# Attention and router kernel on one core: router rows turned on TensorE, a second probabilities' buffer, and norms and tail weighting moved off VectorE

## The chip, the cores and the metric

The kernel runs on one core of a Trainium2 chip. The time is the device time of one execution, in microseconds (us). A core has TensorE (PE in the rows; PEld is its weight load), VectorE (DVE), ScalarE (ACT), GpSimd (POOL) and SyncE (SP), which only issues DMAs. Each engine runs its own list of instructions in order, and the lists are tied together by semaphores that an instruction raises and another engine's instruction waits for.

## What is computed

```python
x = x + xattn(ctx, ctx, layernorm(x))     # 4096 queries of width 512, 3202 keys, one head
x = x + ffn(layernorm(x))                 # 16 experts, the two best of each row, 512 rows an expert at most
# xattn: softmax(q Wq^T (k Wk^T)^T / sqrt(512)) (v Wv^T) Wo^T + biases
# ffn:   gate_probs = softmax(x w_router); each row goes to its two best experts:
#        (silu(x w_gate) * (x w_fc)) w_proj, weighted by the two probabilities
```

## The kernel before

Three blocks run one after the other: `setup` (weights folded into keys `kT` and values `vv`), `attend` (attention and routing, the part that the change touches), and `experts`. `attend` takes the queries in NT = 32 tiles of 128. The 3202 keys are NK = 25 tiles of 128 and a tail of 2. All large products are three passes in f16 of high and low halves (`three_passes`, L45 to L47).

The work is pipelined over steps. In step t:

- TensorE computes the scores of query tile t + 1 (7 chunks of up to 4 key tiles into the banks `sc`), then the tail's scores, then `times_values(t)`: 25 key tiles (k = 0 to 24) of probabilities times values into `acc`. Between these it does small things at fixed places: `row_sum(t)` after k = 0, `greatest(t + 1)` (L1234, the turn of the maxima) after k = 8, `spread(t + 1)` (L1240, the maxima spread to all partitions) after k = 10, `logits(t - 1)` (L1274, L1277, the router's product of tile t - 1) after k = 16. `places(t - 2)` (L1284) stands after the first chunk of scores.
- ScalarE copies the chunks of scores to `s_T` (`copied`, L899), with `rows_high(t - 1)` (L925) after chunk 2 and `query_high(t + 2)` (L936) after chunk 4, then `tail_exp` (L905), the exponentials in three groups of key tiles (L910), and the high halves of the probabilities `pT` (`high`, L919), the last of them after `router_sum(t - 1)` (L929).
- VectorE starts a step with `residual(t - 1)` (L1045 twice, for the two tail keys, and L1048, then the statistics up to L1055). It goes on with the running maximum over the 7 chunks (`maximum`, L999), between which stand `place(t - 2)` (L1104 to L1122, after chunk 1), `normed` and `rows_low(t - 1)` (L1059, L1063, after chunk 2), `row_blocks(t - 1)` (L1067, a transpose in 32 x 32 blocks, after chunk 3) and three parts of `query(t + 2)` (L1128 to L1132, L1135 and L1137, L1140, after chunks 3, 4 and 5). Then come `inverse(t)` (L1029 to L1037), `shift(t + 1)` (the last of the maximum L1004 and L1006, L1008 to L1016, the subtraction L1019 in three groups), `route(t - 1)` (L1086 to L1098) and the low halves of the probabilities (`low`, L1025, three groups).
- GpSimd does `deviation(t - 1)` (L831), `add_bias(t)` (L827: `xb = x_in + bo_row`), `scatter(t - 2)` (L837 to L844, two indirect DMAs), `deviation_q(t + 2)` (L850) and `sums(t + 1)` (L858 six times, L860, L863: the row sums of the exponentials, the first of which waits for the first group of exponentials).
- SyncE loads and stores. The normed rows reach the router transposed through DRAM: `row_blocks` turns 32 x 32 blocks, one DMA stores them to `blocks_r`, and four DMAs load them block by block into `xrT`, which `logits` reads. The queries take the same way through `blocks_q` to `qt`.

So the order on each engine is written out by hand. The places that matter here are these two, `add_bias` before the sums on GpSimd, and the wait at the head of `logits` on TensorE:

```python
if post: deviation(t - 1); add_bias(t)        # GpSimd, step t
if post and placed: scatter(t - 2)
if more_q: deviation_q(t + 2)
if more: sums(t + 1, 1 - h)
...
pe.wait_ge(r_in, 16 * NB * (t + 1))           # TensorE, logits(t)
```

Of the kernel before, what the change touches and what calls it, by code (L numbers as in the profile page):

```python
# [21 lines left out]
ALU = mybir.AluOpType  # L22
# [572 lines left out]
def attend(nc, v):  # L595
# [24 lines left out]
    with ExitStack() as c_:  # L620
# [4 lines left out]
        pT = buf("pT", [P, 2, NK, P], F16)  # L625
# [9 lines left out]
        p_held = buf("p_held", [P, TAIL], F32)  # L635
# [9 lines left out]
        row_bl = buf("row_bl", [P, 2 * D], F16)  # L645
# [40 lines left out]
        ps_y = c_.enter_context(nc.psum_tensor("ps_y", [P, 512], F32))  # L686

# [10 lines left out]
        rb_rdy, rb_out, r_in = sem("rb_rdy"), sem("rb_out"), sem("r_in")  # L698
        qb_rdy, qb_out = sem("qb_rdy"), sem("qb_out")
        rinv_rdy = sem("rinv_rdy")  # L700
# [26 lines left out]
        with nc.Block() as block:  # L727
            @block.sync
            def _(sp):
# [21 lines left out]
                def store_row_blocks(t):  # L751
                    sp.wait_ge(rb_rdy, t + 1)
                    sp.dma_start(blocks_r, row_bl[:]).then_inc(rb_out, 16)

                def load_row_blocks(t):
                    sp.wait_ge(rb_out, 16 * (t + 1))
                    blocks_in(xrT, blocks_r, r_in)

# [13 lines left out]
                def step(t, post, more_x, more_q, turn_q):  # L772
                    if more_x:
                        sp.wait_ge(xb_rdy, t + 1)
                        load_x(t + 1)
                    if post:
                        store_x1(t - 1)
                        store_rows(t - 1)
                        store_row_blocks(t - 1)
                    if more_q:  # L780
                        load_xq(t + 3)
                    if post:
                        load_row_blocks(t - 1)
                    if turn_q:
                        turn_query(t + 2)
# [10 lines left out]
                store_row_blocks(NT - 1)  # L796
                load_row_blocks(NT - 1)
                sp.wait_ge(x1_out, 16 * NT)
                sp.wait_ge(r_out, 16 * NT)
                sp.wait_ge(r_in, 16 * NB * NT)  # L800
# [3 lines left out]
            def _(pool):  # L804
# [71 lines left out]
                add_bias(0)  # L876
# [14 lines left out]
            def _(act):  # L891
# [21 lines left out]
                def high(t, h, g):  # L913

                    a, b = groups[g]
                    act.wait_ge(ex_rdy, NG * t + g + 1)
                    if not isinstance(t, int) or t > 0:
                        act.wait_ge(pv_part, NG * (t - 1) + g + 1)
                    act.activation(pT[:, 0, a:b, :], s_T[h][:, a:b, :], ACT.Copy).then_inc(p_hi, 1)  # L919

                def rows_high(t):
                    act.wait_ge(xs_rdy, t + 1)
                    wait_for(act, r_out, 16 * t)
                    wait_for(act, rb_rdy, t)
                    act.activation(row16[:, 0:D], xs2[:], ACT.Copy, scale=XN_S).then_inc(xs_hi, 1)  # L925
# [7 lines left out]
                def query_high(t):  # L933
                    act.wait_ge(q_xs, t - 1)
                    wait_for(act, qb_rdy, t - 2)
                    act.activation(q16[:, 0:D], xqs[:], ACT.Copy, scale=XN_S).then_inc(q_hi, 1)  # L936

                def step(t, h, post, more, more_q, copies=True):
                    for c in range(NCH if more and copies else 0):
                        copied(t + 1, 1 - h, c)  # L940
                        if c == 2 and post:
                            rows_high(t - 1)
                        if c == 4 and more_q:
                            query_high(t + 2)
                    if post and not more:
                        rows_high(t - 1)
                    if more:
                        tail_exp(t + 1)
                        exponentials(t + 1, 1 - h, 0)
                        exponentials(t + 1, 1 - h, 1)  # L950
                        high(t + 1, 1 - h, 0)
                    if more:
# [33 lines left out]
                rows_high(NT - 1)  # L986
                router_sum(NT - 1)
# [3 lines left out]
            def _(dve):  # L991
# [30 lines left out]
                def low(t, h, g):  # L1022
                    a, b = groups[g]
                    dve.wait_ge(p_hi, NG * t + g + 1)
                    dve.tensor_tensor(pT[:, 1, a:b, :], s_T[h][:, a:b, :], pT[:, 0, a:b, :], ALU.subtract).then_inc(p_lo, 1)  # L1025

                def inverse(t):
                    dve.wait_ge(pt_rdy, t + 1)
                    dve.tensor_tensor(rs_v[:], p_tail[:, 0:1], p_tail[:, 1:2], ALU.add)  # L1029
                    dve.tensor_copy(p_held[:], p_tail[:])  # L1030
# [6 lines left out]
                    dve.reciprocal(rinv[:], rs_v[:]).then_inc(rinv_rdy, 1)  # L1037

                def residual(t):
# [4 lines left out]
                    for i in range(TAIL):  # L1044
                        dve.scalar_tensor_tensor(out=x1[:], in0=v_tail[:, i, :], scalar=p_held[:, i:i + 1],  # L1045
                                                 in1=x1[:] if i else acc[:], op0=ALU.mult, op1=ALU.add)
                        dve.drain()
                    dve.scalar_tensor_tensor(out=x1[:], in0=x1[:], scalar=rinv[:], in1=xb[:],  # L1048
# [6 lines left out]
                    dve.tensor_scalar(var_e[:], mv[:, 1:2], EPS, None, ALU.add).then_inc(mv_rdy, 1)  # L1055

                def normed(t):
                    dve.wait_ge(rs_rdy, t + 1)
                    dve.tensor_scalar(xs2[:], x1[:], mv[:, 0:1], rstd[:], ALU.subtract, ALU.mult).then_inc(xs_rdy, 1)  # L1059

                def rows_low(t):
                    dve.wait_ge(xs_hi, t + 1)
                    dve.scalar_tensor_tensor(out=row16[:, D:2 * D], in0=xs2[:], scalar=XN_S, in1=row16[:, 0:D],  # L1063
                                             op0=ALU.mult, op1=ALU.subtract).then_inc(xs_lo, 1)

                def row_blocks(t):
                    dve.transpose(row_bl[:], row16[:]).then_inc(rb_rdy, 1)  # L1067
# [56 lines left out]
                def query(t, c):  # L1124

                    if c == 3:
                        dve.wait_ge(q_ld, 16 * (t - 1))
# [5 lines left out]
                    if c == 4:  # L1133
                        dve.wait_ge(q_rstd, t - 1)
                        dve.tensor_scalar(shift_q[:], mv_q[:, 0:1], rstd_q[:], 1.0, ALU.mult, ALU.subtract)  # L1135
                        dve.drain()
                        dve.tensor_scalar(xqs[:], xq[:], rstd_q[:], shift_q[:], ALU.mult, ALU.subtract).then_inc(q_xs, 1)  # L1137
# [5 lines left out]
                def step(t, h, post, more, more_q, placed=True):  # L1143
                    if post:
                        residual(t - 1)
                    for c in range(NCH if more else 0):
# [3 lines left out]
                        if c == 2 and post:  # L1150
                            normed(t - 1)
                            rows_low(t - 1)
                        if c == 3 and post:
                            row_blocks(t - 1)
                        if more_q:
                            query(t + 2, c)
                    if not more:
                        place(t - 2)
                        normed(t - 1)
                        rows_low(t - 1)  # L1160
                        dve.drain()
                        row_blocks(t - 1)
# [32 lines left out]
                normed(NT - 1)  # L1195
                rows_low(NT - 1)
                dve.drain()
                row_blocks(NT - 1)
# [7 lines left out]
            def _(pe):  # L1206
# [40 lines left out]
                def times_values(t, post, more):  # L1247
                    wait_for(pe, x1_rdy, t)
                    ends = [b - 1 for a, b in groups]
                    for k in range(NK):  # L1250
# [3 lines left out]
                        last = three_passes(pe, acc[:], (pT[:, 0, k, :], pT[:, 1, k, :]),  # L1254
# [14 lines left out]
                def logits(t):  # L1269

                    pe.wait_ge(r_in, 16 * NB * (t + 1))
# [16 lines left out]
                def step(t, post, more, placed=True):  # L1288
# [8 lines left out]
                    times_values(t, post, more)  # L1297
# [14 lines left out]
                times_values(0, False, True)  # L1312
                step(1, True, True, False)
                with pe.Fori(2, NT - 2) as t:
                    step(t, True, True)
                step(NT - 2, True, True)
                step(NT - 1, True, False)
# [519 lines left out]
```

## Time and profile before

| | us |
|---|---|
| median of three executions | 1792.59 |
| lowest and highest | 1790.32, 1793.38 |
| the profiled execution | 1790.13 |
| its span, first to last instruction | 1788.4 |

| engine | busy, us | share of the span |
|---|---|---|
| TensorE | 1611.5 | 90% |
| VectorE | 1248.5 | 70% |
| ScalarE | 589.9 | 33% |
| GpSimd | 744.9 | 42% |

The span is cut in three: `setup` to about 196 us, `attend` to about 1424 us, `experts` for the rest. A row of a timeline gives the start in us from the span's start, the duration in us, the engine, the line of the kernel, the operation, its output and inputs, how many are merged (x3), and in brackets how long the engine had stood idle before it and whose work ended that wait. A row of a line's instructions gives least, median and greatest duration in ns.

### The profile page before, as it was taken

The page shows a single profiled execution, that of the slowest core. Times are in us where ns is not written, and L with a number is a line of the kernel's source. Part 1 is how long each engine was busy: PE and PEld are TensorE (multiplying, and loading weights), DVE is VectorE, ACT ScalarE, POOL GpSimd, SP SyncE. Part 2 cuts the span into 40 slices and gives each one's busy share as a digit, 9 for nine tenths or more (in the row PEclk, how much of TensorE's full clock was granted, in tenths as well). Part 3 has the DMA queues.
Part 4 walks back from the last instruction along what each step waited for, and adds up shares of the span by engine and source line. Part 5 has one row for each costly group of instructions (what it writes and reads, how often), then busy time and mean ns, then how long its engine had stood idle before and what let it go on. Part 6 is the DMA issues. An engine that isn't in the chain of part 4 may idle for free. (4 is left out here: it accounts for less than half of the span.)

```text
span 1788.4 us, 40760 instructions
## 1 busy us (share of the span) xinstructions
PE 1611.5 (90%) x15565; PEld 1058.9 (59%) x15565; DVE 1248.5 (70%) x2427; ACT 589.9 (33%) x902; POOL 744.9 (42%) x708
## 2 busy tenths in 40 slices
PE   8999989899998999999999899998998369999974
PEld 4444867667766667666776666776665135555430
DVE  4443277888888888888888888888888365555524
ACT  2343233233232332323323233232332025454430
POOL 0100054355443454434544345444455245665540
PEclk9999999999999999999999999999999679999985
DMA  4310112332223322233222322223221268989969
GB/s 153 90 48 7 55 29 66 62 53 47 49 69 59 59 47 47 68 62 59 47 48 70 59 58 47 47 65 64 55 45 37 43 187 186 218 202 217 199 86 375
DMA packets 339922, 155.75 MB, mean 87 GB/s; under 512 B 268642, under 2 KB 285026, under 8 KB 339876
## 3 DMA queue, kind: packets, MB, share of 16 engines
q1 hardware_dynamic: 317424, 111.05, 25.8%
q0 software_dynamic: 16896, 35.42, 10.4%
q10 hardware_dynamic: 5556, 8.66, 1.3%
q8 instruction: 29, 0.48, 0.1%
q14 instruction: 17, 0.14, 0.0%
HBM read 95.04 MB, written 60.06 MB: 87 GB/s over the span
## 5 line engine op out<-in xcount | busy, mean ns | idle before, releaser
L45 PE MATMUL sc<-qt,kT 128*128 128x128 f16 x3100 | 524.5, 219 | 3.8 <-POOL before L821 3.4
L46 PE MATMUL sc<-qt,kT 128*128 128x128 f16 x3100 | 524.4, 219 | 0.0
L47 PE MATMUL sc<-qt,kT 128*128 128x128 f16 x3100 | 524.3, 219 | 0.0
L45 PE MATMUL acc<-vv,pT 128*128 128x512 f16 x800 | 312.7, 391 | 14.3 <-DVE pT L1025 7.8
L46 PE MATMUL acc<-vv,pT 128*128 128x512 f16 x800 | 312.6, 391 | 0.0
L47 PE MATMUL acc<-vv,pT 128*128 128x512 f16 x800 | 312.0, 390 | 0.0
L45 PEld LDWEIGHTS sc<-qt,kT 128*128 128x128 f16 x3100 | 303.6, 98 | 10.4 <-POOL before L821 3.9
L46 PEld LDWEIGHTS sc<-qt,kT 128*128 128x128 f16 x3100 | 303.7, 98 | 3.5
L47 PEld LDWEIGHTS sc<-qt,kT 128*128 128x128 f16 x3100 | 303.7, 98 | 0.0
L858 POOL TENSOR_TENSOR sum<-s_T 128x512 f32<-128x512 f32 x32 | 72.7, 2273 | 378.7 <-ACT s_T L910 378.7
L858 POOL TENSOR_TENSOR sum<-sum,s_T 128x512 f32<-128x512 f32 (+1 forms) x160 | 209.5, 1309 | 31.5 <-issue 16.8
L899 ACT ACTIVATE s_T<-sc 128x512 f32<-128x512 f32 (+1 forms) x224 | 115.3, 541 | 130.4 <-PE sc L47 130.2
L999 DVE TENSOR_TENSOR rm<-rm,s_T 128x512 f32<-128x512 f32 (+1 forms) x160 | 100.5, 628 | 62.5 <-ACT s_T L899 44.7
L1477 POOL DMA_INDIRECT y_dram<-o_sb,sidx x64 | 102.5, 1601 | 99.0 <-ACT o_sb L1520 83.3
L1025 DVE TENSOR_TENSOR pT<-s_T,pT 128x1024 f16<-128x1024 f32 (+1 forms) x96 | 141.0, 1517 | 3.2 <-ACT pT L919 3.2
L910 ACT ACTIVATE s_T<-s_T,e_bias 128x1024 f32<-128x1024 f32 (+1 forms) x96 | 112.8, 1180 | 88.2 <-DVE s_T L1019 88.2
L45 PEld LDWEIGHTS acc<-vv,pT 128*128 128x128 f16 x800 | 84.5, 106 | 94.1 <-issue 14.0
L47 PEld LDWEIGHTS acc<-vv,pT 128*128 128x128 f16 x800 | 80.1, 100 | 100.8 <-issue 11.1
L46 PEld LDWEIGHTS acc<-vv,pT 128*128 128x128 f16 x800 | 79.9, 100 | 80.8 <-issue 5.3
L1019 DVE TENSOR_TENSOR s_T<-s_T,m_b 128x1024 f32<-128x1024 f32 (+1 forms) x96 | 116.1, 1265 | 2.9
L919 ACT ACTIVATE pT<-s_T 128x1024 f16<-128x1024 f32 (+1 forms) x96 | 103.4, 1077 | 1.9 <-PE acc L47 1.9
L844 POOL DMA_INDIRECT tbl_dram<-tok,idx x64 | 73.7, 1151 | 36.7 <-issue 36.7
(292 smaller groups left out, 2849.7 us busy)
## 6 DMA issues: line engine op xcount, KB each, us to landing
xq<-in_x_dram SPq DMA_DIRECT2D x32, 256.0 KB, 2.9
x_in<-in_x_dram SPq DMA_DIRECT2D x32, 256.0 KB, 2.8
raw_g<-in_L_ffn_w_gate_dram SPq DMA_DIRECT2D x16, 512.0 KB
raw_f<-in_L_ffn_w_fc_dram SPq DMA_DIRECT2D x16, 512.0 KB
raw_p<-in_L_ffn_w_proj_dram SPq DMA_DIRECT2D x16, 512.0 KB
y_dram<-x SPq DMA_DIRECT2D x32, 256.0 KB
rows_dram<-row SPq DMA_DIRECT2D x32, 256.0 KB
blocks_r<-row_bl SPq DMA_DIRECT2D x32, 256.0 KB, 2.0
```

Source lines behind the costliest of these rows:

```text
L45: pe.matmul(out, s_hi, m_hi, start=first, stop=False)
L46: pe.matmul(out, s_hi, m_lo, start=False, stop=False)
L47: return pe.matmul(out, s_lo, m_hi, start=False, stop=last)
L844: pool.indirect_dma_start(tbl_dram, bass.IndirectOffsetOnAxis(ap=idx[:, k:k + 1], axis=0), tok[:, k, :], None, bounds_check=2 * E * CAP - ...
L858: pool.tensor_tensor(sum4[:, 0:b - a, :], before_it, s_T[h][:, a:b, :], ALU.add)
L899: act.activation(s_T[h][:, a:b, :].rearrange("p k c -> p (k c)"), sc[c % 3][:, 0:(b - a) * P], ACT.Copy).then_inc(sc_cp, 1)
L910: act.activation(s_T[h][:, a:b, :], s_T[h][:, a:b, :], ACT.Exp, bias=e_bias[:], scale=SM / (XN_S * CTX_S)).then_inc(ex_rdy, 1)
L919: act.activation(pT[:, 0, a:b, :], s_T[h][:, a:b, :], ACT.Copy).then_inc(p_hi, 1)
L999: dve.tensor_tensor(rm[:, 0:b - a, :], so_far, s_T[h][:, a:b, :], ALU.max)
L1019: dve.tensor_tensor(s_T[h][:, a:b, :], s_T[h][:, a:b, :], m_b[:].unsqueeze(1).to_broadcast([P, b - a, P]), ALU.subtract).then_inc(sub_rdy, 1)
L1025: dve.tensor_tensor(pT[:, 1, a:b, :], s_T[h][:, a:b, :], pT[:, 0, a:b, :], ALU.subtract).then_inc(p_lo, 1)
L1477: pool.indirect_dma_start(y_dram, bass.IndirectOffsetOnAxis(ap=sidx[:, e, j:j + 1], axis=0), o_sb[:, e % 2, j, :], None, bounds_check=Y_LA ...
```

## The change

Only `attend` is changed.

- The router's rows are turned on TensorE: `rows_T(t - 1)`, eight transposes of 128 x 128 in f16 after k = 2 of `times_values` (after k = 8 in the last step), into a PSUM bank `turn`; ScalarE copies the bank to `xrT` (`rows_turned`), between `high(t + 1, 0)` and the third group of exponentials. `row_blocks`, the DRAM round trip of the rows and its five DMAs go.
- `pT` becomes two buffers, used in turn, and `high` waits for the values' products of two tiles back. TensorE's loop is unrolled by two for it.
- `normed` leaves VectorE. ScalarE does it in `rows_high`: `xs2 = x1 - mean`, then the high half scaled by `rstd`, which now holds the factor 2^10. VectorE's `residual` gains a small operation for minus the mean.
- The query's norm leaves VectorE: `deviation_q` on GpSimd gains a multiply and a subtract of 128 x 1, and `query_high` on ScalarE the 128 x 512 operation.
- The two tail keys' weighting leaves `residual`: `inverse` ends with `p_rel = p_tail * rinv` (and loses the copy to `p_held`), ScalarE multiplies the two tail values (`tail_values`, two operations of 128 x 512, ahead of `tail_exp`), and GpSimd adds both in `add_bias`, which so has three additions of 128 x 512 with a drain and a wait ahead of the two new ones. `add_bias(t)` now stands at the end of GpSimd's step, behind `sums(t + 1)`.
- SyncE's step has `load_x(t + 1)`, which waits for `add_bias(t)`, at its end.

```diff
-        pT = buf("pT", [P, 2, NK, P], F16)
+        pT = [buf(f"pT{b}", [P, 2, NK, P], F16) for b in range(2)]
...
 def step(t, post, more_x, more_q, turn_q):          # SyncE
+    if post: store_x1(t - 1); store_rows(t - 1)
+    if more_q: load_xq(t + 3)
+    if turn_q: turn_query(t + 2)
     if more_x:
         sp.wait_ge(xb_rdy, t + 1)
         load_x(t + 1)
-    if post: store_x1(t - 1); store_rows(t - 1); store_row_blocks(t - 1)
-    if more_q: load_xq(t + 3)
-    if post: load_row_blocks(t - 1)
-    if turn_q: turn_query(t + 2)
...
 def add_bias(t):                                     # GpSimd
     pool.wait_ge(x_ld, 16 * (t + 1))
     wait_for(pool, x1_rdy, t)
-    pool.tensor_tensor(xb[:], x_in[:], bo_row[:], ALU.add).then_inc(xb_rdy, 1)
+    pool.tensor_tensor(xb[:], x_in[:], bo_row[:], ALU.add)
+    for i in range(TAIL):
+        pool.drain()
+        pool.wait_ge(vr_rdy, TAIL * t + i + 1)
+        added = pool.tensor_tensor(xb[:], xb[:], v_rel[:, i, :], ALU.add)
+    added.then_inc(xb_rdy, 1)
 def deviation_q(t):
     pool.wait_ge(q_var, t - 1)
-    pool.tensor_tensor(rstd_q[:], var_q[:], nhalf[:], ALU.pow).then_inc(q_rstd, 1)
+    pool.tensor_tensor(rstd_q[:], var_q[:], nhalf[:], ALU.pow)
+    pool.drain()
+    pool.tensor_tensor(mr_q[:], mv_q[:, 0:1], rstd_q[:], ALU.mult)
+    pool.drain()
+    pool.tensor_tensor(shift_q[:], ones_f[:, 0:1], mr_q[:], ALU.subtract).then_inc(q_rstd, 1)
 def step(t, h, post, more, more_q, placed=True):
     if post:
         deviation(t - 1)
-        add_bias(t)
...
     if more:
         sums(t + 1, 1 - h)
+    add_bias(t)
...
 def high(t, h, g):                                   # ScalarE
-    act.wait_ge(pv_part, NG * (t - 1) + g + 1)
+    act.wait_ge(pv_part, NG * (t - 2) + g + 1)
 def rows_high(t):
+    act.wait_ge(mv_rdy, t + 1)
+    wait_for(act, r_pe, t)
+    act.activation(xs2[:], x1[:], ACT.Identity, bias=neg_mean[:]).then_inc(xs_rdy, 1)
     act.wait_ge(xs_rdy, t + 1)
+    act.wait_ge(rs_rdy, t + 1)
...
+    act.activation(row16[:, 0:D], xs2[:], ACT.Copy, scale=rstd[:]).then_inc(xs_hi, 1)
+def tail_values(t):
+    act.wait_ge(rinv_rdy, t + 1)
+    wait_for(act, xb_rdy, t)
+    for i in range(TAIL):
+        act.activation(v_rel[:, i, :], v_tail[:, i, :], ACT.Copy, scale=p_rel[:, i:i + 1]).then_inc(vr_rdy, 1)
+def rows_turned(t):
+    act.wait_ge(r_pe, t + 1)
+    wait_for(act, lg_pe, t)
+    act.activation(xrT[:], turn[:], ACT.Copy).then_inc(r_in, 1)
 def query_high(t):
+    act.wait_ge(q_rstd, t - 1)
+    wait_for(act, qb_rdy, t - 2)
+    act.activation(xqs[:], xq[:], ACT.Identity, bias=shift_q[:], scale=rstd_q[:]).then_inc(q_xs, 1)
 # in step: tail_values(t) ahead of tail_exp(t + 1)
         high(t + 1, 1 - h, 0)
+    if post:
+        rows_turned(t - 1)
     if more:
         exponentials(t + 1, 1 - h, 2)
...
 def inverse(t):                                      # VectorE
-    dve.tensor_copy(p_held[:], p_tail[:])
...
+    dve.tensor_scalar(p_rel[:], p_tail[:], rinv[:], None, ALU.mult).then_inc(rinv_rdy, 1)
 def residual(t):
-    for i in range(TAIL):
-        dve.scalar_tensor_tensor(out=x1[:], in0=v_tail[:, i, :], scalar=p_held[:, i:i + 1], ...)
...
-def normed(t): ...
-def row_blocks(t): ...
-    # in query, after chunk 4: shift_q and xqs
...
+def rows_T(t):                                       # TensorE
+    pe.wait_ge(xs_lo, t + 1)
+    wait_for(pe, r_in, t)
+    for k in range(2 * KT):
+        last = pe.transpose(turn[:, k, :], row16[:, k * P:(k + 1) * P], ident16[:])
+    last.then_inc(r_pe, 1)
 # in times_values:
+    if post and k == (2 if more else 8):
+        rows_T(t - 1)
 def logits(t):
-    pe.wait_ge(r_in, 16 * NB * (t + 1))
+    pe.wait_ge(r_in, t + 1)
```

## Rows read from the trace of the kernel before

**Rows 1.** Waits of TensorE from 279 to 1326 us: total, times, longest

```profile
PE ps_x L1234 <- DVE rm L1006: 63.8, 27, 2.6
```

**Rows 2.** Line L1234 from 278 to 1330 us: durations in ns, first and last start

```profile
L1234 PE MATMUL ps_x<-ident,rm x29: 272/329/476, 279.0 to 1326.6; 128*128 128x128 f32 x29
```

**Rows 3.** Timeline of TensorE, two steps

```profile
616.87 0.33 PE L1234 MATMUL ps_x<-ident,rm 128*128 128x128 f32 x1 [2.25 <-DVE rm L1006]
...
622.43 0.25 PE L1274 MATMUL ps_m<-w_r,xrT 128*128 128x32 f16 x4
...
653.71 0.33 PE L1234 MATMUL ps_x<-ident,rm 128*128 128x128 f32 x1 [2.47 <-DVE rm L1006]
...
656.30 0.63 PE L1240 MATMUL ps_y<-diag,ones_f 128*128 128x128 f32 x2
```

**Rows 4.** Timeline of VectorE, the same stretch

```profile
619.44 3.63 DVE L1019 TENSOR_TENSOR s_T<-s_T,m_b 128x1024 f32<-128x1024 f32 x3
622.98 0.17 DVE L1086 TENSOR_SCALAR lg<-ps_m 128x16 f32<-128x16 f32 x1
...
630.17 4.41 DVE L1025 TENSOR_TENSOR pT<-s_T,pT 128x1024 f16<-128x1024 f32 x3
634.50 0.73 DVE L1045 SCALAR_TENSOR_TENSOR x<-v_tail,p_held,acc 128x512 f32<-128x512 f32 x1
...
639.39 0.78 DVE L1106 TENSOR_TENSOR P<-e_two,P 128x1 f32 x1 [0.28 <-issue]
...
641.29 0.16 DVE L1122 TENSOR_TENSOR ia<-ia,ib 128x2 f32<-128x2 f32 x1
...
642.25 0.54 DVE L1059 TENSOR_SCALAR xs<-x,mvb,rstdb 128x512 f32<-128x512 f32 x1
643.62 0.69 DVE L1063 SCALAR_TENSOR_TENSOR row<-xs,row 128x512 f16<-128x512 f32 x1 [0.83 <-ACT row L925]
...
645.08 1.24 DVE L1067 STREAM_TRANSPOSE row_bl<-row 128x1024 f16<-128x1024 f16 x1
...
647.23 0.15 DVE L1132 TENSOR_SCALAR var_q<-mv_q 128x1 f32<-128x1 f32 x1
...
650.17 0.69 DVE L999 TENSOR_TENSOR rm<-rm,s_T 128x512 f32<-128x512 f32 x1 [1.18 <-ACT s_T L899]
...
657.35 3.63 DVE L1019 TENSOR_TENSOR s_T<-s_T,m_b 128x1024 f32<-128x1024 f32 x3
```

**Rows 5.** Timeline of ScalarE, the same stretch

```profile
622.89 1.04 ACT L919 ACTIVATE pT<-s_T 128x1024 f16<-128x1024 f32 x1
...
649.02 0.63 ACT L936 ACTIVATE q<-xqs 128x512 f16<-128x512 f32 x1 [4.46 <-DVE xqs L1137]
```

**Rows 6.** Timeline of GpSimd, the same stretch

```profile
621.92 2.27 POOL L858 TENSOR_TENSOR sum<-s_T 128x512 f32<-128x512 f32 x1 [10.73 <-ACT s_T L910]
...
633.51 1.39 POOL L863 TENSOR_TENSOR sum<-sum 128x128 f32<-128x128 f32 x1
...
645.51 0.97 POOL L844 DMA_INDIRECT tbl_dram<-tok,idx  x1 [0.30 <-issue]
```

**Rows 7.** GpSimd's lines over the whole span: durations in ns, least, median, greatest

```profile
L858 POOL TENSOR_TENSOR sum<-sum,s_T x160: 452/1269/2213, 226.3 to 1375.1; 128x512 f32<-128x512 f32 x128, 128x128 f32<-128x128 f32 x32
L860 POOL TENSOR_TENSOR sum<-sum x32: 722/1521/1527, 233.8 to 1376.6; 128x256 f32<-128x256 f32 x32
L827 POOL TENSOR_TENSOR xb<-x_in,bo_row x32: 1251/1408/1421, 196.8 to 1383.6; 128x512 f32<-128x512 f32 x32
```

**Rows 8.** Groups of GpSimd, 279 to 1326 us: busy us, mean ns, idle before

```profile
L837 POOL TENSOR_TENSOR idf<-ia,ic 128x2 f32<-128x2 f32 x28 | 5.5, 195 | 39.2 <-DVE ia L1122 39.2
```

**Rows 9.** TensorE's transposes in `experts`, timeline

```profile
1475.61 1.06 PE L1741 MATMUL tp<-ident,rows 128*128 128x128 f16 x16
```

**Rows 10.** ScalarE's copies of such turned rows, durations in ns

```profile
L1513 ACT ACTIVATE xTe<-tp x32: 1014/1023/1023, 1441.8 to 1705.5; 128x1024 f16<-128x1024 f16 x32
```

**Rows 11.** The last router product, TensorE's timeline

```profile
1417.53 0.29 PE L1274 MATMUL ps_m<-w_r,xrT 128*128 128x32 f16 x4 [16.05 <-DMA xrT<-blocks_r]
```

More of the change, by code:

```diff
@@ L634, in attend @@
         p_tail = buf("p_tail", [P, TAIL], F32)
-        p_held = buf("p_held", [P, TAIL], F32)
+        p_rel = buf("p_rel", [P, TAIL], F32)
+        v_rel = buf("v_rel", [P, TAIL, D], F32)
+        neg_mean = buf("neg_mean", [P, 1], F32)
+        mr_q = buf("mr_q", [P, 1], F32)
         sum4 = buf("sum4", [P, CH, P], F32)
@@ L686, in attend @@
         ps_y = c_.enter_context(nc.psum_tensor("ps_y", [P, 512], F32))
+        turn = c_.enter_context(nc.psum_tensor("turn", [P, 2 * KT, P], F16))
         a_const = sem("a_const")
@@ L772, in step @@
                 def step(t, post, more_x, more_q, turn_q):
+                    if post:
+                        store_x1(t - 1)
+                        store_rows(t - 1)
+                    if more_q:
+                        load_xq(t + 3)
+                    if turn_q:
+                        turn_query(t + 2)
                     if more_x:
@@ L874, in step @@
                         sums(t + 1, 1 - h)
-                add_bias(0)
+                    add_bias(t)
                 sums(0, 0)
@@ L946, in step @@
                         rows_high(t - 1)
+                        tail_values(t)
                     if more:
+                        tail_values(t)
                         tail_exp(t + 1)
@@ L986, in _ @@
                 rows_high(NT - 1)
+                rows_turned(NT - 1)
                 router_sum(NT - 1)
@@ L1036, in inverse @@
                     dve.drain()
-                    dve.reciprocal(rinv[:], rs_v[:]).then_inc(rinv_rdy, 1)
+                    dve.reciprocal(rinv[:], rs_v[:])
+                    dve.drain()
+                    wait_for(dve, vr_rdy, TAIL * t)
+                    dve.tensor_scalar(p_rel[:], p_tail[:], rinv[:], None, ALU.mult).then_inc(rinv_rdy, 1)
                 def residual(t):
@@ L1043, in residual @@
                     wait_for(dve, x1_out, 16 * t)
-                    for i in range(TAIL):
[L1045 to L1048, printed above, removed]
+                    wait_for(dve, xs_rdy, t)
+                    dve.scalar_tensor_tensor(out=x1[:], in0=acc[:], scalar=rinv[:], in1=xb[:],
                                              op0=ALU.mult, op1=ALU.add).then_inc(x1_rdy, 1)
@@ L1054, in residual @@
                     dve.drain()
[L1055 to L1059, printed above, removed]
+                    dve.tensor_scalar(neg_mean[:], mv[:, 0:1], -1.0, None, ALU.mult)
+                    dve.tensor_scalar(var_e[:], mv[:, 1:2], EPS, XN_S ** -2, ALU.add, ALU.mult).then_inc(mv_rdy, 1)
                 def rows_low(t):
                     dve.wait_ge(xs_hi, t + 1)
-                    dve.scalar_tensor_tensor(out=row16[:, D:2 * D], in0=xs2[:], scalar=XN_S, in1=row16[:, 0:D],
+                    dve.scalar_tensor_tensor(out=row16[:, D:2 * D], in0=xs2[:], scalar=rstd[:], in1=row16[:, 0:D],
                                              op0=ALU.mult, op1=ALU.subtract).then_inc(xs_lo, 1)
-                def row_blocks(t):
-                    dve.transpose(row_bl[:], row16[:]).then_inc(rb_rdy, 1)
                 def query_blocks(t):
@@ L1126, in query @@
                     if c == 3:
+                        wait_for(dve, q_xs, t - 2)
                         dve.wait_ge(q_ld, 16 * (t - 1))
@@ L1150, in step @@
                         if c == 2 and post:
[L1151 to L1154, printed above, removed]
+                                rows_low(t - 1)
                         if more_q:
@@ L1245, in row_sum, with times_values @@
                     pe.matmul(ps_y[:, P:P + 1], sum1[:], ones_f[:, 0:1], start=True, stop=True).then_inc(rs_pe, 1)
-                def times_values(t, post, more):
+                def rows_T(t):
[4 more added lines that the diff above has]
+                    last.then_inc(r_pe, 1)
+                def times_values(t, h, post, more):
                     wait_for(pe, x1_rdy, t)
@@ L1253, in times_values @@
                                 pe.wait_ge(p_lo, NG * t + g + 1)
-                        last = three_passes(pe, acc[:], (pT[:, 0, k, :], pT[:, 1, k, :]),
+                        last = three_passes(pe, acc[:], (pT[h][:, 0, k, :], pT[h][:, 1, k, :]),
                                             (vv[:, k, 0, :], vv[:, k, 1, :]), k == 0, k == NK - 1)
@@ L1286, in places, with step @@
                               start=False, stop=True).then_inc(pos_pe, 1)
-                def step(t, post, more, placed=True):
+                def step(t, h, post, more, placed=True):
                     for c in range(NCH if more else 0):
@@ L1296, in step @@
                         places(t - 2)
-                    times_values(t, post, more)
+                    times_values(t, h, post, more)
                 pe.wait_ge(a_const, 13)
@@ L1311, in _ @@
                 pe.wait_ge(wr_lo, 1)
[L1312 to L1317, printed above, removed]
+                times_values(0, 0, False, True)
+                step(1, 1, True, True, False)
+                with pe.Fori(1, NT // 2 - 1) as m:
+                    for h in range(2):
+                        step(2 * m + h, h, True, True)
+                step(NT - 2, 0, True, True)
+                step(NT - 1, 1, True, False)
+                rows_T(NT - 1)
                 logits(NT - 1)
```

45 lines of the change are left out of this document (6 added, 39 removed).

## The prediction

> **What bounds the kernel now.** I read the waits of TensorE first, then the starts of one line that comes once a step, then the timelines of two steps. In the 28 steps between 279 and 1326 us TensorE has one recurring wait: at L1234, the turn of the maxima after k = 8, it waits for VectorE's last maximum, 63.8 us in all [rows 1]. L1234 starts 29 times from 279.0 to 1326.6, so a step lasts 37.41 on average [rows 2]. The step shown lasts 653.71 - 616.87 = 36.84, with a wait of 2.25 [rows 3]. So TensorE's own work is 36.84 - 2.25 = 34.59 a step, and the step is set by a loop that runs mostly through VectorE. I name three points of it: A, where L1019 (the subtraction of the maxima) starts; R, where `residual` starts; G, where L1234 starts.
>
> - A to R: 634.50 - 619.44 = 15.06 [rows 4]: subtraction, `route`, `low`, with no wait.
> - R to G: 653.71 - 634.50 = 19.21 [rows 3, 4]: `residual`, the seven maxima and what stands between them, `inverse`.
> - G to the next A: 619.44 - 616.87 = 2.57 [rows 3, 4].
>
> They add up to 36.84. After the second wait the spread L1240 takes 0.63 [rows 3] and A comes 657.35 - 653.71 = 3.64 after G [rows 3, 4], 1.07 later than after the first. I read this as the granted clock falling from 2.4 to 1.2 GHz for a moment after TensorE's idle time. Such steps make the average 37.41 - 36.84 = 0.57 longer than the clean step.
>
> **What VectorE loses.** From R to G: two tail operations, 0.73 with a drain each, 1.6 in all; the norm and the wait behind it, 643.62 - 642.25 = 1.37; the block transpose, 1.2 [rows 4]. L1106 took 0.78 beside GpSimd's `add_bias`; with that addition moved away it should take about the 0.16 of its neighbours, 0.6 less [rows 4]. Added are minus the mean and `p_rel`, against the lost copy: 0.07 and 0.17, priced as a drain and a small operation. Had these been all, the loop would fall below TensorE's 34.59. They are not, since the work moved lands on two other engines at places that the same loop passes.
>
> **A to R, `add_bias` behind the sums.** `residual(t)` waits for `xb`, which GpSimd now makes after `sums(t + 1)`. The sums start at 621.92 = A + 2.48 and end at 633.51 + 1.39 = 634.90 = A + 15.46 [rows 4, 6], already 0.4 behind R. Three additions follow at 1.25 to 1.41 each [rows 7].
>
> The sums get shorter first. The last three (L858's 128 x 128, L860, L863) lie beside `low`. L863 took 1.39 there [rows 6], where the same shape has taken 0.45, and L860 usually 1.52 where it has taken 0.72 [rows 7]. I read this as the two engines taking turns, whole instructions at a time. `low` now starts later (next part), so these three run alone: 0.95 + 0.8 + 0.95 = 2.7 less, and the sums end at A + 12.8.
>
> Then the three additions of 128 x 512 meet the three operations of `low`. If they take turns, what is left from A + 12.3, the start of `low`, is the last sum of 0.45, three additions of 1.25 [rows 7], and `low` without its waits, for which I take the 3.63 of L1019's three groups of the same size [rows 4]: 12.3 + 0.45 + 3.75 + 3.63 = 20.1. R moves from A + 15.06 to about A + 20.0. If they did not disturb each other it would be 12.8 + 3 x 1.4 = A + 17.0, which is the lower bound; the upper is 15.46 + 3 x 1.8 = A + 20.9, with the additions as slow as the slowed neighbours. I take 20.0, since the rows show turns. That the waiting engine stands for the whole of the other's instruction is also what the Trainium skill says (SBUF — State Buffer, Who interferes with whom): a VectorE operation with two SBUF inputs and a GpSimd one that reads SBUF block each other fully. The trace agrees with 1.39 against 0.45.
>
> **A to R, the router's rows.** TensorE reaches `logits` at 622.43 = A + 2.99 [rows 3, 4]. Now it waits there for ScalarE's `rows_turned`, which is queued behind two groups of exponentials and `high(0)`; `high(0)` ends at 622.89 + 1.04 = A + 4.49 [rows 5], and the copy costs 1.02 [rows 10]: A + 5.5. That is a new wait of 2.5 on TensorE, with the eight last key tiles and the next scores behind it. `route` waits for the product and starts at A + 6.0 instead of 622.98 = A + 3.54 [rows 4]. It lasted 630.17 - 622.98 = 7.19 [rows 4] beside long additions; with the short sums at its end I take 6.3, so `low` starts at A + 12.3.
>
> **R to G, the query.** The order on GpSimd decides. The index of `scatter` was ready at 641.45 = R + 6.95 and is now at R + 4.8 (1.6 and 0.6 less, 0.07 more). The scatter's last DMA ended at 645.51 + 0.97, 5.03 after the index [rows 4, 6], so now at R + 9.8. The query's variance was ready at 647.38 = R + 12.88 [rows 4] and is now ready at 12.88 - 1.6 - 0.6 - 1.37 - 1.2 + 0.07 = R + 8.2. So `deviation_q` starts at R + 9.8, behind the scatter. From the variance to ScalarE's L936 it took 649.02 - 647.38 = 1.64 [rows 4, 5]; the same work now has two GpSimd operations of 0.2 [rows 8] with drains in place of VectorE's one, and a hand-over more: 2.05. L936 starts at R + 11.85. Behind it on ScalarE is the copy of chunk 5, for whose maximum VectorE waits: 650.17 - 649.02 = 1.15 [rows 4, 5], R + 13.0. From there to G it was 653.71 - 650.17 = 3.54, now 3.7 with `p_rel`: G at R + 16.7, against 19.21. The lower bound is 15.2, if the scatter held up nothing; the upper is 17.5.
>
> **The sum.** 20.0 + 16.7 + 2.57 = 39.27; with the roughness of the two places I take 39.2, which is 2.35 more a step than 36.84, under the same average for the clock. Over 28 steps: 66. TensorE's 34.59, plus 0.53 for eight transposes (half of 1.06) [rows 9], plus the wait of 2.5, is 37.6, below 39.2: so L1234 still waits, about 1.6, and the transposes themselves cost nothing as long as that wait covers them (0.53 a step if it is gone). The doubled `pT` I cost at nothing: no wait for it recurs in [rows 1]. SyncE's `load_x` moved to the end lands most of a step before it is needed: nothing. `tail_values`, two operations near ScalarE's 0.63 [rows 5], lies in the time in which ScalarE waits for `shift`: nothing.
>
> At the ends: the last router product waited 16.05, most of it the block transpose and two DMA trips [rows 11]; a transpose of 0.53 and a copy of 1.02 replace them, 8.5 less, and 1.5 less for the tile before. The last two steps and the first, where `residual` also waits for the later `xb`, give back 6 (an estimate from the 5 of R). Net -4. From the profiled execution: 1790.1 + 66 - 4 = 1852; the median of the runs is 2.5 above it: **1854**.
>
> **Rivals.**
> - TensorE takes over. If `xb` is ready by A + 18.3 (no turns between additions and `low`), the loop falls under 37.6 and TensorE sets the step with its new wait at `logits`: 37.6, or 38.2 with the clock's 0.57, against 37.41. 28 x 0.2 to 0.8, less 4: 1797 to 1813, point 1807, with the best end at 1789. For it: the lower bound of 17.0. Against it: the slowed sums.
> - Faster. Both new waits hide: ScalarE finishes the turned rows by k = 16 and `xb` comes by R. TensorE then sets 34.59 + 0.53 = 35.1: 28 x -2.3, less 8: 1720. It decides at ScalarE's place at A + 3.0, where the rows have it in the exponentials. The Trainium skill speaks for this side (Perfetto Trace Analysis, Optimizing Scalar/DVE Operations): with VectorE saturated, handing work to ScalarE or even GpSimd may help, though the shared port may spoil it. By it the time is this 1720.
> - Slower still. TensorE now idles twice a step, and the clock falls after every wait, 1.07 each instead of 0.57 on average: 14 more, 1868.
> - The change does not do what it says, for instance the compiler's loop or queues swallow it: 1790.
>
> **How the numbers follow.** Forecast 0.57, slower still 0.15, TensorE takes over 0.15 (0.10 of it slower, 0.03 the same, 0.02 faster), faster 0.10, no effect 0.03. So slower by over 0.2% 0.82, within 0.2% 0.06, faster 0.12; 0.2%, 3.6 us, is about what a measurement of this kernel can tell from none. The range from 1798 to 1876 takes in the forecast with both ends of its bounds at R (A + 20.9 gives 1876), the slower case and most of TensorE's.
>
> **What would show it.** In the profile after: VectorE's first operation of `residual` waits for GpSimd, 2 to 3 us a step; the third addition ends near A + 20; TensorE waits about 2.5 at L1274's counterpart for ScalarE's copy and less than before at the turn of the maxima; VectorE's maximum of chunk 5 waits about 4 for ScalarE, which waits for GpSimd's subtraction behind the scatter. Wrong would be: no wait at `residual` (then TensorE's rival), or the turned rows in `xrT` before TensorE gets there (then the faster one).

## The result and the profile after

| | before | after |
|---|---|---|
| median, us | 1791.45 (4 runs) | 1889.64 (4 runs) |
| ratio to before, 95% interval | | 1.055 (1.053 to 1.057) |
| span of the profiled execution | 1788.4 | 1890.4 |
| VectorE busy, share | 1248.5 (70%) | 1110.1 (59%) |
| ScalarE busy | 589.9 | 720.2 |
| GpSimd busy | 744.9 | 860.5 |

VectorE lost 138 us of work, and the kernel became 98 us slower. The direction was forecast, the size was not: the forecast was 1854, with a range from 1798 to 1876.

Waits of TensorE after, 279 to 1420 us (total, times, longest), where [rows 1] had one recurring wait:

```profile
PE ps_x L1232 <- DVE rm L1024: 62.6, 28, 3.7
PE ps_m L1281 <- ACT xrT L936: 60.8, 28, 2.3
```

The same of VectorE:

```profile
DVE rm L1017 <- ACT s_T L896: 140.4, 29, 5.4
DVE x L1065 <- POOL xb L820: 80.8, 28, 2.9
DVE lg L1097 <- PE ps_m L1284: 64.1, 28, 2.3
```

The turn of the maxima (durations in ns, first and last start), to be held against [rows 2]:

```profile
L1232 PE MATMUL ps_x<-ident,rm x29: 327/329/476, 281.2 to 1428.7; 128*128 128x128 f32 x29
```

(1428.7 - 281.2) / 28 = 40.98 us a step, against 37.41. So 28 x 3.57 = 100 us are the steps of the loop. The rest of the 102 between the two spans is 2 net: the first of these starts comes 2.2 later, the last step grows from 35.6 to 39.9, and what follows the last turn of the maxima, where the DRAM round trip is gone, is 4.3 shorter.

One step after, VectorE's timeline; A, R and G as in the prediction, [rows 4] has the lines of before:

```profile
612.43 3.63 DVE L1037 TENSOR_TENSOR s_T<-s_T,m_b 128x1024 f32<-128x1024 f32 x3
618.35 0.17 DVE L1097 TENSOR_SCALAR lg<-ps_m 128x16 f32<-128x16 f32 x1 [2.29 <-PE ps_m L1284]
...
624.45 4.95 DVE L1043 TENSOR_TENSOR pT<-s_T,pT 128x1024 f16<-128x1024 f32 x3
632.29 0.75 DVE L1065 SCALAR_TENSOR_TENSOR x<-acc,rinv,xb 128x512 f32<-128x512 f32 x1 [2.89 <-POOL xb L820]
...
636.92 0.16 DVE L1133 TENSOR_TENSOR ia<-ia,ib 128x2 f32<-128x2 f32 x1
...
640.39 0.15 DVE L1144 TENSOR_SCALAR var_q<-mv_q 128x1 f32<-128x1 f32 x1
...
646.58 0.69 DVE L1017 TENSOR_TENSOR rm<-rm,s_T 128x512 f32<-128x512 f32 x1 [5.17 <-ACT s_T L896]
```

and GpSimd's, against [rows 6]:

```profile
625.94 2.24 POOL L816 TENSOR_TENSOR xb<-x_in,bo_row 128x512 f32<-128x512 f32 x1
628.39 2.14 POOL L820 TENSOR_TENSOR xb<-xb,v_rel 128x512 f32<-128x512 f32 x1 [0.21 <-issue]
630.74 1.27 POOL L820 TENSOR_TENSOR xb<-xb,v_rel 128x512 f32<-128x512 f32 x1 [0.21 <-issue]
...
641.70 0.98 POOL L838 DMA_INDIRECT tbl_dram<-tok,idx  x1 [0.30 <-issue]
642.70 0.59 POOL L844 TENSOR_TENSOR rstd_q<-var_q,nhalf 128x1 f32<-128x1 f32 x1
644.04 0.19 POOL L846 TENSOR_TENSOR mr_q<-mv_q,rstd_q 128x1 f32<-128x1 f32 x1 [0.75 <-issue]
```

and TensorE's and ScalarE's:

```profile
609.86 0.33 PE L1232 MATMUL ps_x<-ident,rm 128*128 128x128 f32 x1 [1.78 <-DVE rm L1024]
...
617.89 0.27 PE L1281 MATMUL ps_m<-w_r,xrT 128*128 128x32 f16 x4 [2.30 <-ACT xrT L936]
...
650.43 0.48 PE L1232 MATMUL ps_x<-ident,rm 128*128 128x128 f32 x1 [2.22 <-DVE rm L1024]
```

```profile
616.83 1.00 ACT L936 ACTIVATE xrT<-turn 128x1024 f16<-128x1024 f16 x1
...
644.59 0.81 ACT L947 ACTIVATE xqs<-xq,shift_q,rstd_q 128x512 f32<-128x512 f32 x1 [5.68 <-POOL shift_q L848]
645.44 0.63 ACT L949 ACTIVATE q<-xqs 128x512 f16<-128x512 f32 x1
```

R is now 632.29 - 612.43 = 19.86 after A (before 15.06), because VectorE waits 2.89 for GpSimd's third addition. Beside `low` the first two additions take 2.24 and 2.14; the third, alone, takes 1.27. G comes 650.43 - 632.29 = 18.14 after R (before 19.21), with a new wait in it: VectorE waits 5.17 for ScalarE's copy of chunk 5, before which ScalarE waits 5.68 for GpSimd's subtraction, which stands behind the scatter. With 612.43 - 609.86 = 2.57 from G to A the clean step is 40.57.

### The profile page after: what moved, and what is told of

It reads as the page before. It is cut to its first block and busy times, and to the rows that moved or that the text cites. A ratio compares the mean times of both kernels' runs of the same rounds, so it can differ in the third digit from the quotient of the medians.

```text
span 1890.4 us, 41563 instructions
## 1 busy us (share of the span) xinstructions
PE 1658.1 (88%) x15821; PEld 1078.1 (57%) x15821; DVE 1110.1 (59%) x2271; ACT 720.2 (38%) x1060; POOL 860.5 (46%) x832
## 3 DMA queue, kind: packets, MB, share of 16 engines
q1 hardware_dynamic: 179696, 94.27, 18.1%
## 5 line engine op out<-in xcount | busy, mean ns | idle before, releaser
L45 PE MATMUL acc<-vv,pT 128*128 128x512 f16 x800 | 323.7, 405 | 12.1 <-DVE x L1065 7.8
L46 PE MATMUL acc<-vv,pT 128*128 128x512 f16 x800 | 322.6, 403 | 0.0
L47 PE MATMUL acc<-vv,pT 128*128 128x512 f16 x800 | 322.4, 403 | 0.0
L896 ACT ACTIVATE s_T<-sc 128x512 f32<-128x512 f32 (+1 forms) x224 | 119.4, 547 | 243.5 <-PE sc L47 243.2
L856 POOL TENSOR_TENSOR sum<-sum,s_T 128x512 f32<-128x512 f32 (+1 forms) x160 | 181.1, 1132 | 26.8 <-issue 12.3
L1043 DVE TENSOR_TENSOR pT<-s_T,pT 128x1024 f16<-128x1024 f32 (+1 forms) x96 | 158.6, 1701 | 1.7 <-ACT pT L916 1.7
L47 PEld LDWEIGHTS acc<-vv,pT 128*128 128x128 f16 x800 | 82.3, 103 | 107.5 <-issue 22.9
L45 PEld LDWEIGHTS acc<-vv,pT 128*128 128x128 f16 x800 | 86.8, 108 | 95.0 <-issue 22.9
L46 PEld LDWEIGHTS acc<-vv,pT 128*128 128x128 f16 x800 | 82.3, 103 | 84.0 <-issue 18.3
L820 POOL TENSOR_TENSOR xb<-xb,v_rel 128x512 f32<-128x512 f32 x64 | 107.5, 1680 | 13.0 <-issue 12.0
```

The lines of the kernel that those rows point to most:

```text
L45: pe.matmul(out, s_hi, m_hi, start=first, stop=False)
L46: pe.matmul(out, s_hi, m_lo, start=False, stop=False)
L47: return pe.matmul(out, s_lo, m_hi, start=False, stop=last)
L820: added = pool.tensor_tensor(xb[:], xb[:], v_rel[:, i, :], ALU.add)
L856: pool.tensor_tensor(sum4[:, 0:b - a, :], before_it, s_T[h][:, a:b, :], ALU.add)
L896: act.activation(s_T[h][:, a:b, :].rearrange("p k c -> p (k c)"), sc[c % 3][:, 0:(b - a) * P], ACT.Copy).then_inc(sc_cp, 1)
```

## The experiments

Steps are the mean of the 29 intervals between the starts of the turn of the maxima from the third tile's on, 37.35 before and 40.94 after. Each kernel is the changed kernel with the edit shown, unless its text says otherwise. A ratio is to the kernel before as measured again beside that kernel, so its time is not always the 1791.45 above.

| kernel | median, us | ratio to before (95%) | step, us |
|---|---|---|---|
| the change | 1889.6 | 1.055 (1.053 to 1.057) | 40.94 |
| query ahead of the scatter | 1814.6 | 1.013 (1.011 to 1.015) | 38.43 |
| `add_bias` ahead of the sums | 1813.4 | 1.013 (1.011 to 1.015) | 38.56 |
| rows copied early | 1893.9 | 1.058 (1.056 to 1.060) | 41.24 |
| all three | 1730.2 | 0.966 (0.964 to 0.968) | 35.69 |
| before, turn alone, late copy | 1791.3 | 1.000 (0.999 to 1.001) | 37.51 |
| before, turn alone, early copy | 1743.6 | 0.973 (0.971 to 0.975) | 36.07 |
| all three, one `pT` | 1701.7 | 0.950 (0.948 to 0.951) | 34.77 |
| tail weighting undone | 1830.6 | 1.022 (1.020 to 1.024) | 38.96 |
| all three, one `pT`, loop of two | 1732.7 | 0.965 (0.963 to 0.968) | 35.78 |
| the change, one `pT` | 1888.6 | 1.052 (1.050 to 1.055) | 40.89 |
| query's norm undone | 1842.3 | 1.028 (1.025 to 1.030) | 39.37 |

**The query ahead of the scatter.**

```diff
+                    if more_q:
+                        deviation_q(t + 2)
                     if post and placed:
                         scatter(t - 2)
-                    if more_q:
-                        deviation_q(t + 2)
```

> The changed kernel with deviation_q ahead of scatter on GpSimd. Theory (the loop through VectorE, and its piece from residual to the turn of the maxima, sets the step; this piece is long because the query's norm waits on GpSimd behind the scatter): the pow starts 2.1 us earlier after residual, the piece falls from 18.1 to 16.0, the clean step from 40.6 to 38.4, the time from 1889 to about 1830. Rival (the step is set by TensorE's two waits and the clock, or by the chain through xb alone): under 10 us of change, 1880 to 1890.

Measured: 75 us less, more than the 60 expected. GpSimd's timeline in it:

```profile
614.49 0.55 POOL L844 TENSOR_TENSOR rstd_q<-var_q,nhalf 128x1 f32<-128x1 f32 x1 [5.59 <-DVE var_q L1144]
615.17 0.19 POOL L846 TENSOR_TENSOR mr_q<-mv_q,rstd_q 128x1 f32<-128x1 f32 x1
615.51 0.19 POOL L848 TENSOR_TENSOR shift_q<-ones_f,mr_q 128x1 f32<-128x1 f32 x1
```

The pow now waits for the variance, not for the scatter, and the 0.75 between pow and multiply is down to 615.17 - 615.04 = 0.13: the drain between them cost 0.75 only where it stood right behind the indirect DMAs. The piece from R to VectorE's read of the turned maxima falls from 18.5 to 16.3 (medians over the steps). `residual` still waits for the additions (77.9 us in 27 times from 279 to 1300 us, 2.9 each time, as before the edit), and TensorE's wait at the maxima falls to 6.5 us in all. So this piece did close the loop. The gain is larger than expected in the main because slow stretches of TensorE go with the wait: in the change A comes more than 3 us after G, at the lower clock, in 10 of the 29 steps, here in none.

**`add_bias` ahead of the sums.**

```diff
+                    add_bias(t)
                     if more:
                         sums(t + 1, 1 - h)
-                    add_bias(t)
```

> The changed kernel with add_bias(t) ahead of sums(t+1) on GpSimd, three additions as before. Theory (residual waits for the additions behind the sums): they now lie in GpSimd's idle time before the sums, residual starts at the end of low, about 16 us after the subtraction instead of 19.9; the loop falls to about 36.9 and TensorE with its wait at logits takes over at 37.3 (37.7 with the clock): 1799. Rival (the additions slow VectorE wherever they stand, the place is of no account): 1870 or more.

A to R falls from 19.8 to 15.8 (medians), as expected, and the wait at `residual` is gone; the place of the additions was the cost. TensorE then sets the step with its wait at `logits`. The time is 14 us above what I expected. The shortest steps are 36.9, the expected kind; most are 38.6 and more. TensorE's timeline of one of these shows the main reason:

```profile
667.20 0.49 PE L1238 MATMUL ps_y<-diag,ones_f 128*128 128x128 f32 x2 [0.39 <-DVE diag L1028]
...
674.15 0.27 PE L1281 MATMUL ps_m<-w_r,xrT 128*128 128x32 f16 x4 [2.58 <-ACT xrT L936]
...
676.97 0.63 PE L45 MATMUL acc<-vv,pT 128*128 128x512 f16 x1
```

Soon after the wait the products of 512 columns take 0.63 and not 0.38, and the mean granted clock from 674 to 684 us is 0.83: part of this stretch runs at the lower of the two levels, 1.2 GHz. With VectorE ahead of TensorE nothing absorbs that time. Nine times from 279 to 1300 us TensorE also stands for up to 1.1 us amid the scores with nothing to wait for (6.8 us in all); the runs with one buffer, below, bear on such stops.

**The turned rows copied early.**

```diff
                         tail_exp(t + 1)
+                        if post:
+                            rows_turned(t - 1)
                         exponentials(t + 1, 1 - h, 0)
 ...
-                    if post:
+                    if post and not more:
                         rows_turned(t - 1)
```

> The changed kernel with the copy of the turned rows ahead of the exponentials on ScalarE. Theory (the new wait at logits is real but the loop is closed by the additions behind the sums, which start at the same time as before): TensorE's wait of 2.2 us at logits goes, route starts 2.3 us earlier, but low then meets the last sums again and residual still starts near 19.7 us after the subtraction; the wait at the turn of the maxima grows by what the one at logits gave; 1880, at best 1870. Rival (the wait at logits is what the slower step is made of): 2.2 us a step less, 1825 to 1830.

Measured: no gain at all; its interval overlaps that of the change. TensorE's waits, 279 to 1326 us (its lines are two further down here, so this is the turn of the maxima):

```profile
PE ps_x L1234 <- DVE rm L1026: 111.4, 26, 6.1
```

The wait at `logits` is gone, and the one at the maxima has grown from about 2.2 to 4.3 a step. The rival, that the wait at `logits` is what makes the step long, is out: with the loop closed elsewhere it only moves. A to R and R to G are what they were (19.7 and 18.1, medians). The few tenths a step that I expected went with the clock, whose mean is 0.94 from 279 to 1300 us here against 0.96 in the change: after the one long wait A comes more than 3 us after G in 23 of 29 steps, against 10 in the change.

**All three.**

> The three edits together. Theory: the loop through VectorE is 15.1 + 16.0 + 2.6 = 33.7 us, below TensorE's own 34.6 plus 0.5 for the transposes; TensorE has no wait in a step, the step is 35.1 to 35.4 and the time about 1727, faster than both kernels. Rival (GpSimd's extra operations and the port cost VectorE more than the removed work in any order): the wait at the turn of the maxima stays and the time is above 1760.

Measured as expected, 1730 and a step of 35.69: the same work on the same engines as in the change, in another order, is 159 us faster than the change and 60 faster than before. TensorE's waits at `logits` and at the maxima are gone (2.5 us in all at the maxima).

**The turn alone, on the kernel before.** The router's rows turned on TensorE and no other part of the change; first with the copy where the change has it, then ahead of the exponentials.

> The kernel before with the router's rows turned on TensorE alone, the copy at the change's place. Theory: VectorE's block transpose goes (1.2 us less between residual and the turn of the maxima), but the wait at logits comes (2.2 us) and route and low are later by about 1.5 us; the loop is 16.6 + 18.0 + 2.6 = 37.2, TensorE's with its wait 37.3; with 8 us less at the end 1785 to 1812, about 1795, so nearly the time before. Rival (the DRAM round trip and the transpose were a cost by themselves): 1750 to 1760 here already.

> The same, with the copy of the turned rows ahead of the exponentials. Theory: no wait at logits, the loop is 15.1 + 18.0 + 2.6 = 35.7, 1.2 a step less than before, and 8 less at the end: about 1750. Rival (the place of the copy is of no account): the same as with the late copy.

Both as expected: 1791.3, no difference from before, and 1743.6. In the first TensorE has one recurring wait, for the copy, from 279 to 1326 us:

```profile
PE ps_m L1269 <- ACT xrT L917: 64.3, 28, 2.3
```

Removing the block transpose and the DRAM trip is worth 48 us, and the place of one copy of 1.0 us on ScalarE eats all of it.

**One buffer of probabilities.**

```diff
-        pT = [buf(f"pT{b}", [P, 2, NK, P], F16) for b in range(2)]
+        pT = buf("pT", [P, 2, NK, P], F16)
 ...
-                        act.wait_ge(pv_part, NG * (t - 2) + g + 1)
+                        act.wait_ge(pv_part, NG * (t - 1) + g + 1)
 ...
-                with pe.Fori(1, NT // 2 - 1) as m:
-                    for h in range(2):
-                        step(2 * m + h, h, True, True)
+                with pe.Fori(2, NT - 2) as t:
+                    step(t, 0, True, True)
```

> The kernel with all three edits and a single buffer of probabilities again, TensorE's loop of one step. Theory (the second buffer is worth nothing): 1730 within 3 us, or up to 8 us less, since TensorE's loop is half as long and its short waits for nothing visible (12 us) may go. Rival (the second buffer is what lets the steps be this short): 1740 or more, with ScalarE's high halves waiting for the values' products.

> The kernel with all three edits and one buffer of probabilities, but TensorE's loop again of two steps. Theory (the 28 us between the two kernels of all three edits, 1730 with two buffers and 1702 with one, are the longer loop, whose instructions are fetched anew: 149 packets of instructions against 29): 1730. Rival (the second buffer itself costs or the wait on it does): 1702.

> The changed kernel with one buffer of probabilities and TensorE's loop of one step, nothing else. Theory (the step is closed by the loop through VectorE, ScalarE and GpSimd, and TensorE waits 4.4 us a step, which covers the fetched instructions): at most 8 us less, 1881 to 1890. Rival (the longer loop is a quarter of the loss): 1862.

The first surprised me: 1701.7, 28 us less, where I had expected 8 at most. Every step but one lies between 34.7 and 34.8. The profile's rows of the instruction queue (packets, MB, share of the DMA engines), first with the loop of two steps (all three edits, two buffers), then with the loop of one:

```profile
q8 instruction: 149, 2.44, 0.6%
```

```profile
q8 instruction: 29, 0.48, 0.1%
```

and TensorE's waits in the first of these two, 279 to 1300 us:

```profile
PE sc L47 <- issue: 11.8, 13, 1.4
PE sc L45 <- DMA qt<-blocks_q: 7.7, 13, 1.0
```

13 times in this stretch, about once in each round of the loop, TensorE stands for about 0.9 us with nothing to wait for, in the middle of the scores, and 13 times at their start, for the queries' DMA; with the loop of one the first wait is gone and the second is 0.2 us, once. With one buffer and the loop of two (1732.7) the loss is back. So it is the loop, not the buffer. The 120 packets more are between eight and nine for each of the loop's 14 rounds, so I read the row as a body of two steps that is fetched anew in each round, and a body of one step that is not; that the stops are waits for these packets was not seen directly. In the change itself one buffer with the short loop changes nothing that can be told (1888.6 against 1889.6), since TensorE waits there anyway. The second buffer is worth nothing that can be told where it was tried alone (1730.2 with it, 1732.7 without, both with the loop of two); that its loop costs nothing is true only under the cover of other waits.

The kernel with the turn alone and the early copy (1743.6) also has one buffer and the short loop. Against it the norms and the tail's weighting, with their places mended, are worth the rest of the way to 1701.7, 42 us.

**The tail's weighting undone** (`residual` and `add_bias` as in the kernel before, the rest as in the change).

> The changed kernel with the tail's weighting back in residual and add_bias back ahead of the scatter. Theory (two places close the loop): residual starts about 16.6 us after the subtraction instead of 19.9, but the index of the scatter is ready 2.2 us later after residual, and the query waits behind the scatter as before, so that piece grows from 18.1 to 20.3; step 39.5 clean, about 1860. Rival (the additions behind the sums are the only cause): the step goes back to 36.9 or less, 1790.

The rival is out, since the step stays above that of before. My number was 30 us too high. In this trace R comes 15.8 after A and not 16.6, which is 22 of them. R to G is 20.3 (median), as expected. The steps are 38.4 to 38.7 and, every second time, longer, up to 40.4. In most of the long ones the drain behind the scatter holds GpSimd for longer, up to 2.3 us (32.1 us in 28 times, where the usual 0.75 would make 21); a few are long without it, and what makes it long was not found.

**The query's norm undone** (the norm back on VectorE, GpSimd with the pow alone, still behind the scatter).

> The changed kernel with the query's norm back on VectorE and its two small operations off GpSimd; deviation_q still stands behind the scatter. Theory (my price for that chain was too low by the drain of 0.75 on GpSimd and by ScalarE's slower operation): from the scatter's end to ScalarE's high half of the query 1.1 to 1.3 us less, so as much less a step, 1853 to 1859. Rival (the position behind the scatter alone is the cost): 1885 or more.

The pow still stands behind the scatter:

```profile
626.40 0.97 POOL L838 DMA_INDIRECT tbl_dram<-tok,idx  x1 [0.30 <-issue]
627.38 0.60 POOL L844 TENSOR_TENSOR rstd_q<-var_q,nhalf 128x1 f32<-128x1 f32 x1
```

```profile
628.88 0.63 ACT L943 ACTIVATE q<-xqs 128x512 f16<-128x512 f32 x1 [5.12 <-DVE xqs L1142]
```

From the pow's start to ScalarE's high half it takes 628.88 - 627.38 = 1.50, where the change takes 645.44 - 642.70 = 2.74. That is the expected 1.2, and the clean step is 39.36. The time falls by 47, more than the 31 to 36 expected, for the reason seen with the query ahead of the scatter: with a shorter wait at the maxima, the slow stretches after it (10 of 29 steps in the change) are gone but for one.

## Why the prediction was wrong in size

- **The loop and its three pieces.** Right. Waits appeared at the three places named, and the kernels with one edit and with all three show that it is one loop: one place mended alone gives nothing (the copy), or stops at the next bound (the other two).
- **A to R.** Forecast 20.0, measured 19.86. The turns between GpSimd and `low` are there, as read from [rows 6, 7]; the parts fit less well than the sum. The sums ended at A + 13.6 and not 12.8, since the last of them met `low` (1.40 instead of 0.45), while the third addition ran alone. The lower bound, no turns, was wrong, and so was the rival that rested on it.
- **The wait at `logits`.** Forecast 2.5, measured 2.3. It adds nothing to the time of the change, as the sum had it.
- **R to G.** This is the step that failed: forecast 16.7, measured 18.14, and beyond its upper bound of 17.5. The order of things was right (the pow behind the scatter, chunk 5 behind the query). Three prices in it were too low, and the query's chain most of all. From the pow's start to ScalarE's high half it was 2.74, not 2.05, with 0.75 of drain behind the indirect DMAs, and with 0.81 for ScalarE's operation where the 1.64 taken over from the kernel before held VectorE's of 0.55 (first row below). The run with the query's norm undone shows this term by itself: 1.24 less. The scatter ended 642.68 - 637.08 = 5.60 after its index, not 5.03. Two of its small operations took 0.72 each (last two rows), ending with VectorE's beside them, where before they took about 0.2 (second and third row); its first DMA operation was 0.5 shorter. The last piece, from the maximum of chunk 5 to G, was 650.43 - 646.58 = 3.85, not 3.7.

```profile
648.44 0.55 DVE L1137 TENSOR_SCALAR xqs<-xq,rstd_q,shift_q 128x512 f32<-128x512 f32 x1
642.31 0.18 POOL L839 COPY tok<-P 128x2 f32 x1
642.63 0.20 POOL L841 CAST idx<-idf 128x2 int32<-128x2 f32 x1
...
637.93 0.72 POOL L833 COPY tok<-P 128x2 f32 x1
638.78 0.72 POOL L835 CAST idx<-idf 128x2 int32<-128x2 f32 x1
```

The prediction priced new small operations by the busy time of their like and had no row for a drain behind a DMA; the bound should have been wider there. 28 x 1.4 is 40 us, and the forecast was short by 36.
- **The range.** It took in one upper bound at a time. 17.5 for R to G gives 28 x 0.8 more, the 1876; A + 20.9 gives 28 x 0.9, 1879 and not 1876; both together give 1901, which would have held the measured time. In the rival in which TensorE takes over, the low end comes to 1794 and not 1797. Neither slip moves the forecast itself.
- **The clock.** I took 0.57 a step over; it was 40.98 - 40.57 = 0.41.
- **The ends.** Forecast 4 less, measured 2 more. The 6 that were to be given back were a guess and came close: 2.2 + 4.3. The 10 less at the end did not come in full: it was 4.3. From the last operation of the last `residual` to the last router product it is now 1519.03 - 1512.44 = 6.59, before 1417.53 - 1404.45 = 13.08, so 6.5 less there and not 8.5 (the eight transposes took 1.03, not 0.53), and 1.6 of it was lost on the way from the last turn of the maxima to that `residual`.
- **The doubled buffer at nothing.** Right for the time of the change (1888.6 with one buffer), wrong as a statement on the kernel: 28 to 31 us once TensorE sets the step. I had looked for a wait that the buffer would remove and not at what the unrolled loop adds.
- **The faster rival.** 1720 was what both waits hidden, the copy's and that for `xb`, would give. With the query moved ahead of the scatter as well, 1730 was measured with the change's loop and 1702 with the short one. The two edits without the third were not run; R to G, at 18.1 in the change, would still be in the loop. The Trainium skill says that, if VectorE is saturated, handing some work to ScalarE or even GpSimd may make sense (Perfetto Trace Analysis, Optimizing Scalar/DVE Operations). VectorE was busy for 70% of the span here, and the measured gain came only with the places changed; at the change's places the time was 98 us longer.

## What to carry to other kernels

In this kernel the place in the new engine's queue decided what moved work cost, from 98 us more to about 60 us less than before, with the same operations on the same engines. Price an operation at the moment at which its consumer needs it, with all that stands ahead of it. Where several new waits lie on one loop, mend them together before judging any one of them; alone, each of the three looks like half a gain or none. When a loop is unrolled for a buffer, look at the instruction queue's row. When the pieces of a sum each have an upper bound, add them before giving the range.

## What the runs showed of the hardware

- With two indirect DMAs just ahead, the drain between GpSimd's pow and its multiply mostly held it for 0.75 us or more (20.6 us in 27 times in the change; up to 2.4 with `add_bias` ahead of the sums and 2.3 with the tail's weighting undone), against 0.13 where the DMAs came after.
- TensorE's loop with two steps in its body took 149 packets of instructions against 29 with one step, and cost 28 to 31 us in a kernel whose step TensorE sets.
- ScalarE's 128 x 512 operation on SBUF took 0.63 with a constant scale [rows 5]; in the change it took 0.72 with one operand per partition (L921, L925) and 0.81 with two (L947).
- VectorE and GpSimd held each other up where both read two tiles from SBUF: additions that take 1.27 to 1.28 where none lies beside `low` (the kernel with all three edits) took 2.24 and 2.14 beside it. The sum of A to R fits a reading in which the later instruction waits for the whole of the earlier.
